# Packing the first attention's small matmuls into quarter tiles, and a new order at two seams

## The reference, cut to what matters

```
def _L0_xattn_ref(x, cond, ...):          # x, cond: (16, 64, 512): 64 channels, 512 positions
    HEADS, WINDOW = 8, 16                 # 8 channels a head
    q, k, v = Wq x + bq, Wk cond + bk, Wv cond + bv        # over the 64 channels
    k, v = padded by 8 positions on the left and 7 on the right
    # each position t attends to its window of 16 positions, t-8 .. t+7
    dots = einsum('bhdt,bhdtw->bhtw', q, k_windows) * 8 ** -0.5
    attn = softmax(dots)
    out = einsum('bhtw,bhdtw->bhdt', attn, v_windows)
    return Wo out + bo
x = x + _L0_xattn_ref(_layernorm(x), ctx, ...)
x = x + _L0_ffn_ref(_layernorm(x), ...)   # rounds its input to int8 steps, gate and up, silu, rounds, down
```

## Time and profile before

| | |
|---|---|
| median of 3 runs | 1571.63 us (1570.21 to 1572.16) |
| the profiled execution | 1569.83 us, its span 1568.0 us |
| busy in the span | PE 1493.3, DVE 820.6, ACT 749.3, POOL 502.2 us |
| instructions | 27690 |
| first attention | from about 12 us (first scores) to about 230 us |

### The profile page before, as it was taken

The page is one execution under the profiler, slowest core; times in us unless marked ns, Lnnn a source line. Parts: engine busy times, 40 slices in busy tenths (PEclk is TensorE's granted clock), DMA queues, the critical chain, the costliest instruction groups (busy, mean ns, idle before and its releaser), DMA issues. The chain is left out here.

```text
span 1568.0 us, 27690 instructions
## 1 busy us (share of the span) xinstructions
PE 1493.3 (95%) x10396; PEld 1240.2 (79%) x10402; DVE 820.6 (52%) x1682; ACT 749.3 (48%) x2552; POOL 502.2 (32%) x656
## 2 busy tenths in 40 slices
PE   7988979999999999999999998779999999999998
PEld 6777768888989888888889887656666778888876
DVE  4767875544444555544443457666665412343465
ACT  5645545454545445454544565355433312455552
POOL 6677652322222212222222224245322000123334
PEclk9999999999999999999999999999999999999999
DMA  8000010020100101010010110010100001122111
GB/s 256 10 9 15 2 41 29 30 73 28 41 27 4 38 28 42 28 41 28 7 36 28 41 55 1 21 64 0 41 1 0 9 23 55 47 70 80 46 27 63
DMA packets 44453, 58.20 MB, mean 37 GB/s; under 512 B 25488, under 2 KB 32672, under 8 KB 41504
## 3 DMA queue, kind: packets, MB, share of 16 engines
q1 hardware_dynamic: 43872, 56.05, 11.3%
q10 hardware_dynamic: 384, 0.38, 0.1%
q0 software_dynamic: 64, 0.00, 0.0%
HBM read 48.81 MB, written 2.10 MB: 32 GB/s over the span
## 5 line engine op out<-in xcount | busy, mean ns | idle before, releaser
L1862 ACT ACTIVATE big<-pb 128x128 f32<-128x128 f32 x384 | 106.7, 278 | 298.5 <-PE pb L902 195.8
L2232 POOL TENSOR_TENSOR big<-big 128x512 f32<-128x512 f32 x96 | 100.0, 1042 | 258.3 <-DVE big L1494 258.3
L1911 ACT ACTIVATE big<-pb,big 128x128 f32<-128x128 f32 x384 | 136.1, 368 | 57.0 <-issue 34.3
L1489 DVE TENSOR_REDUCE big<-pb 128x4 f32<-128x512 f32 x96 | 65.8, 686 | 176.1 <-PE pb L941 168.1
L917 PE MATMUL pb<-wkh,CXh 128*128 128x256 f32 x512 | 149.7, 292 | 0.0
L2222 POOL TENSOR_SCALAR big<-big 128x6 f32<-128x6 f32 x64 | 12.9, 202 | 412.8 <-ACT big L1862 412.2
L917 PE MATMUL pb<-wkl,CXh 128*128 128x256 f32 x512 | 145.0, 283 | 0.0
L917 PE MATMUL pb<-wkh,CXl 128*128 128x256 f32 x512 | 144.2, 282 | 0.0
L1280 DVE TENSOR_TENSOR X<-X,pb 128x512 f32<-128x512 f32 x128 | 87.0, 679 | 79.7 <-PE pb L1128 39.3
L968 PE MATMUL pb<-woh,oh 128*128 128x512 f32 x256 | 113.0, 442 | 0.0
L902 PE MATMUL pb<-wqh,CXh 128*128 128x512 f32 x256 | 101.8, 397 | 3.0 <-DVE big L1459 1.6
(11 more groups left out here) (283 smaller groups left out, 3872.7 us busy)
## 6 DMA issues: line engine op xcount, KB each, us to landing
big<-in_w SPq DMA_DIRECT2D x17, 1024.0 KB, 5.0
big<-in_w SPq DMA_DIRECT2D x24, 256.0 KB, 3.0
big<-in_w SPq DMA_DIRECT2D x8, 512.0 KB, 3.6
o<-o SPq DMA_DIRECT2D x96, 32.0 KB, 1.9
X<-in_x SPq DMA_DIRECT2D x8, 256.0 KB, 4.8
big<-in_cn SPq DMA_DIRECT2D x8, 256.0 KB, 3.0
CXlf<-in_cT SPq DMA_DIRECT2D x8, 256.0 KB, 5.1
big<-in_wa SPq DMA_DIRECT2D x1, 2048.0 KB, 8.6
```

The lines of the kernel that those rows point to most:

```text
L1489: v.tensor_reduce(m[j % 2], quarters(bank(p)), AX, MAX, negate=True).then_inc(S.m, 1)
L1862: y = a.activation(sq[i % 2], bank(p)[:, j * width:j * width + 128], ACT.Square, accum_out=ss[i % 2][:, first + j:first + j + 1])
L1911: y = a.activation(e_[:, c], bank(p)[:, c], ACT.Exp, bias=m[j % 2][:, k:k + 1], scale=1.0, accum_out=z[j % 2][:, k:k + 1])
L2232: g.tensor_tensor(quarters(e_), quarters(e_), bc(r[j % 2], 128), MUL).then_inc(*on.to(S.pn))
```

## The change

The list `l0` gets two PE stages, `l0_half` and `l0_second`, around `l0_turn`. Together they compute the scores of unit u and the values of unit u+1 as matmuls of 64x64: in the first half, 8 of the scores on the diagonal quarters and 8 of the values off it; in the second half the other way round. The other engines' stages `l0_scores` and `l0_project` keep their places; PE does `l0_project` only for unit 0. The weighing takes the heads one by one (32 matmuls with 32 columns of weights and 32 moving columns in place of 16 with 64 and 64), so that only 128 columns of a bank are filled and copied; the output takes two heads at a time (2 matmuls in place of 4). The two pipeline steps of the feed-forward block stand at 9 and 11 of the longer list, ahead of `l0_scores` and of `l0_norm` as before. Stages of `ffn1` get `first`: `f1_stats`, `f1_norm`, `f1_turn` and `f1_mm` come ahead of `l2_turn`, `l2_rows`, `l2_stats` and `f1_quant` in their pipeline step. Weights, masks and their host layout follow (channels in another order); two bias products on ACT go.

```diff
-    l0 = [("l0_mask", 2), ("l0_rows", 1), ("l0_out", 7), ("l0_sum", 4), ("l0_ctx", 7), ("l0_weigh", 6), ("l0_turn", 5),
-          ("l0_scores", 3), ("l0_project", 2), ("l0_norm", 0), ("l0_qk", 1)]
+    l0 = [("l0_mask", 2), ("l0_rows", 1), ("l0_out", 7), ("l0_sum", 4), ("l0_ctx", 7), ("l0_weigh", 6), ("l0_half", 3),
+          ("l0_turn", 5), ("l0_second", 3), ("l0_scores", 3), ("l0_project", 2), ("l0_norm", 0), ("l0_qk", 1)]
...
-    ffn1 = pipeline([3 * t for t in range(NT)], [(s, None if s == "f1_wait" else every) for s in f1])
+    ffn1 = pipeline([3 * t for t in range(NT)], [(s, None if s == "f1_wait" else every) for s in f1],
+                    first=("f1_stats", "f1_norm", "f1_turn", "f1_mm"))
...
-            together(next(att0), (ffn0, 7), (ffn0, 9))
+            together(next(att0), (ffn0, 9), (ffn0, 11))
...
-        together(first[:7], (late, 6), (ffn0, 7))
+        together(first[:9], (late, 7), (ffn0, 9))
...
+            halves = slice(0, 64), slice(64, 128)
+
+            def pad_values(u):
+                g, p = u % 4, PSUM["l0_project", u, "v"]
+                return pe.matmul(bank(p)[:, g * 128:g * 128 + 128], pad[0:16, g // 3 * 128:g // 3 * 128 + 128],
+                                 pad[0:16, 256:384], start=False, stop=True, skip_group_check=True)
+
+            def values(u, k, rows_, keys, first):
+                n = rows_ * 16
+                return pe.matmul(view(bank(PSUM["l0_project", u, "v"])[halves[keys]], k * 128 + n, [[32, 4], [1, 16]]),
+                                 CP[u % 3][halves[rows_], k * 128 + keys * 64:k * 128 + keys * 64 + 64],
+                                 view(wv0[halves[rows_]], n, [[32, 4], [1, 16]]), start=first, stop=True,
+                                 skip_group_check=True)
+
+            def scores(u, i, rows_, out_):
+                t, g = divmod(u, 4)
+                return pe.matmul(bank(PSUM["l0_scores", u, "S"])[halves[out_], i * 64:i * 64 + 64],
+                                 Qx[u % 2][halves[rows_], i * 64:i * 64 + 64],
+                                 view(K0[t % 2][halves[rows_]], (8 * g + i) * 16, [[560, 2], [1, 32]]), start=False,
+                                 stop=True, skip_group_check=True)
+
             def l0_project(u):
-                t, g = divmod(u, 4)
+                if u:
+                    return
                 on.wait_ge(D.w0, 16)
                 on.wait_ge(D.pad, 16)
                 p = PSUM["l0_project", u, "v"]
-                C_ = CP[u % 3]
                 on.wait_ge(S.cp, 2 * u + 2)
                 on.wait_ge(p.free, p.n)
                 for k in range(4):
-                    a = pe.matmul(bank(p)[:, k * 128:k * 128 + 128], C_[:, k * 128:k * 128 + 128], wv0,
-                                  start=(k == 0), stop=True, skip_group_check=True)
-
-                if g in (0, 3):
-                    a = pe.matmul(bank(p)[:, g * 128:g * 128 + 128], pad[0:16, g // 3 * 128:g // 3 * 128 + 128],
-                                  pad[0:16, 256:384], start=False, stop=True, skip_group_check=True)
-                a.then_inc(p.full, 1)
-
-            def l0_scores(u):
+                    pe.matmul(bank(p)[:, k * 128:k * 128 + 128], CP[u % 3][:, k * 128:k * 128 + 128], wv0,
+                              start=(k == 0), stop=True, skip_group_check=True)
+                pad_values(u).then_inc(p.full, 1)
+
+            def l0_half(u):
                 t, g = divmod(u, 4)
                 p, k = PSUM["l0_scores", u, "S"], PSUM["l0_qk", 4 * t, "k"]
                 on.wait_ge(S.qx, u + 1)
                 on.wait_ge(k.free, k.n + 1)
                 on.wait_ge(S.band, 2)
                 on.wait_ge(p.free, p.n)
-                halves = slice(0, 64), slice(64, 128)
                 for r in halves:
                     pe.matmul(bank(p)[r], bandb[r, 0:64], bandb[r, 128:640], start=True, stop=False, skip_group_check=True)
-                for i in range(8):
-                    for r in halves:
-                        a = pe.matmul(bank(p)[r, i * 64:i * 64 + 64], Qx[u % 2][r, i * 64:i * 64 + 64],
-                                      view(K0[t % 2][r], (8 * g + i) * 16, [[560, 2], [1, 32]]), start=False,
-                                      stop=True, skip_group_check=True)
-                a.then_inc(p.full, 1)
+                if u + 1 < 4 * NT:
+                    v = PSUM["l0_project", u + 1, "v"]
+                    on.wait_ge(S.cp, 2 * u + 4)
+                    on.wait_ge(v.free, v.n)
+                for i in range(4):
+                    for r in range(2):
+                        a = scores(u, i, r, r)
+                        if i == 3:
+                            a.then_inc(S.half0, 1)
+                    for r in range(2):
+                        if u + 1 < 4 * NT:
+                            a = values(u + 1, i, r, 1 - r, i == 0)
+                            if i == 3:
+                                a.then_inc(S.half0, 1)
+
+            def l0_second(u):
+                p = PSUM["l0_scores", u, "S"]
+                on.wait_ge(S.half0, 4 * u + (4 if u + 1 < 4 * NT else 2))
+                for i in range(4):
+                    for r in range(2):
+                        a = scores(u, 4 + i, r, 1 - r)
+                    if i == 3:
+                        a.then_inc(p.full, 1)
+                    for r in range(2):
+                        if u + 1 < 4 * NT:
+                            a = values(u + 1, i, r, r, False)
+                if u + 1 < 4 * NT:
+                    if (u + 1) % 4 in (0, 3):
+                        a = pad_values(u + 1)
+                    a.then_inc(PSUM["l0_project", u + 1, "v"].full, 1)
 
...
                 for j in range(4):
                     for p, r in zip((p0, p1), halves):
-                        for c in halves:
-                            k = slice(j * 128 + c.start, j * 128 + c.stop)
-                            a = pe.matmul(bank(p)[c, j * 64:j * 64 + 64], VW[u % 4][r, k], PT0[u % 2][r, k],
+                        for h in range(4):
+                            c = j * 128 + 32 * ((h + j // 2 * 2) % 4)
+                            a = pe.matmul(bank(p)[32 * h:32 * h + 32, j * 32:j * 32 + 32],
+                                          VW[u % 4][r, j * 128 + 32 * h:j * 128 + 32 * h + 32], PT0[u % 2][r, c:c + 32],
...
-                for h in range(4):
+                for h in range(2):
                     a = pe.matmul(bank(p)[:, 0:128], wo0[:, h, :],
-                                  view(AV[u % 2], h * 16, [[64, 4], [256, 2], [1, 16]]), start=(h == 0), stop=(h == 3))
+                                  view(AV[u % 2], h * 16, [[32, 4], [128, 2], [1, 16]]), start=(h == 0), stop=(h == 1))
...
-                    a.copy(AV[u % 2][:, h * 256:h * 256 + 256], bank(p)[:, 0:256]).then_inc(p.free, 1)
+                    a.copy(AV[u % 2][:, h * 128:h * 128 + 128], bank(p)[:, 0:128]).then_inc(p.free, 1)
```

More of the change, by code:

```diff
@@ L414, in build_program @@
         S.zero, S.zp, S.two = sem("dve_constants"), sem("pool_constants"), sem("l0_wo_masked")
-        S.cp, S.qx, S.band = sem("l0_windows"), sem("l0_q_masked"), sem("l0_band")
+        S.cp, S.qx, S.band, S.half0 = sem("l0_windows"), sem("l0_q_masked"), sem("l0_band"), sem("l0_first_half")
         S.exp0, S.rc0, S.pn0 = sem("l0_exp"), sem("l0_reciprocal"), sem("l0_probs")
@@ L588, in build_program @@
         K0 = [b.rearrange("p (b n) -> p b n", b=2) for b in Kbd]
-        wo0 = al(4 * 128).rearrange("p (h n) -> p h n", h=4)
+        wo0 = al(2 * 128).rearrange("p (h n) -> p h n", h=2)
         bo0 = al(1)
@@ L592, in build_program @@
         al = carve(R1, R1 + 6144)
-        Qx, VW, AV = slots(al, 2, 512), slots(al, 4, 512), slots(al, 2, 512)
+        Qx, VW, AV = slots(al, 2, 512), slots(al, 4, 512), slots(al, 2, 256)
         al = carve(R1 + 6144, R1 + 10240)
@@ L599, in build_program @@
         pad, bandb = al(384), al(640, BF16)
-        wo_raw, band = CXf[0][:, 64:198], CXf[0][:, 2048:2688]
-        wob, bv0, hmo, bo_raw = wo_raw[:, 0:128], wo_raw[:, 128:129], wo_raw[:, 129:133], wo_raw[:, 133:134]
+        wo_raw, band = CXf[0][:, 64:196], CXf[0][:, 2048:2688]
+        wob, bv0, hmo, bo_raw = wo_raw[:, 0:128], wo_raw[:, 128:129], wo_raw[:, 129:131], wo_raw[:, 131:132]
         al = carve(RF, R0 + 22788)
@@ L1226, in f3_mm @@
                 a.then_inc(p.full, 1)
-            do = dict(l0_bias=l0_bias, l0_qk=l0_qk, l0_project=l0_project, l0_scores=l0_scores, l0_turn=l0_turn,
+            do = dict(l0_bias=l0_bias, l0_qk=l0_qk, l0_project=l0_project, l0_half=l0_half, l0_second=l0_second, l0_turn=l0_turn,
                       l0_weigh=l0_weigh, l0_out=l0_out, f0_turn=f0_turn, f0_turn_u=f0_turn_u, f0_gate=f0_gate, f0_turn2=f0_turn2, f0_down=f0_down,
@@ L2525, in diag @@
         return z
-    order = np.arange(128).reshape(2, 2, 32).transpose(1, 0, 2).reshape(128)
+    order = np.arange(128).reshape(2, 4, 16).transpose(1, 0, 2).reshape(128)
     p = np.arange(128)
```

(7 more changed lines are left out.)

## The result

The changed kernel takes 1611.12 us (median of 4 runs, 1606.5 to 1617.1) against 1570.92 for the kernel before on the same chip: ratio 1.0257, interval 1.0235 to 1.0278. It is slower, by 40 us where the forecast had 23; its median lies 2 to 3 us above the range (1577 to 1609 in the sum, 1576 to 1608 in the chances). The profiled execution's span is 1607.5 us.

A forecast was written before the change was run, and what follows sets the result against it. The prediction took the first feed-forward's ring across engines, not PE's busy share, as the bound; 1.8 + 19.2 + 7 - 5 = +23 us on 1571.63 gave 1594 us, range 1577 to 1609 (1576 to 1608 in the chances).

The forecast's parts named there:

- The bank-0 wait: First half of unit 4t+10 waits for ACT's quT copy out of bank 0: 3.2 us a tile, +19.2 us.
- The clock: PE stands still before quT's end, clock falls to half speed: 1.2 us a tile, +7 us (0 to 10).
- the 4.8 us: Predicted time from quT's end to DVE's gate step in each tile, against 1.3 us today.
- The start: First units' halves wait bare for ACT's copy of the values: +1.8 us (0.4 to 2.5).
- The seam: Near 1000 us, second feed-forward's stages go ahead of layer 2's turn: -5 us (-9 to +3).
- Saved TensorE time: PE work removed per attention unit: 1.3 us, 40 us over 31 units, counted as nothing.
- the ring: First feed-forward layer's closed loop through POOL, DVE, ACT and PE, once per tile, 29.1 us; said to set the time.
- Rival 1: PE is the bound after all: 15 us of the 40 and 5 from the seam gained, 1552; chance 0.09.
- rival 2: The waits are hidden by slack or earlier ACT copies; only start and seam count: 1568; chance 0.10.
- Weighing in 64 records: PE's new weighing in 32-column tiles: taken as 0.63 us; by record rate 1.26, by the skill page 1.6.
- the two waits: PE's halves wait for ACT's values copy in every unit (+1.8 us) and for quT in every tile (+19.2 us).

The follow-up runs named there:

- e4: The changed kernel with unread bf16 matmuls put into TensorE's longest standstills of the first attention, no wait removed: 1594.3 us, ratio 1.0145.
- e5: The changed kernel with l0_project ahead of l0_scores, so ACT copies the values before the exponential: 1604.0 us, ratio 1.0212.
- e1: The kernel before with only the order of stages in the second feed-forward's pipeline at the seam changed: 1566.5 us, ratio 0.9968.
- e9: The changed kernel with values copied before the exponential and both halves back to back where the scores stood: 1568.8 us, ratio 0.9984.
- e12: The changed kernel with only both halves moved back to back behind the turn and the feed-forward's stages: 1580.8 us, ratio 1.0067.
- e6: The changed kernel with values copied before the exponential and f0_turn_u of tiles 0 to 5 in bank 1: 1594.0 us, ratio 1.0148.
- e2: The changed kernel with f0_turn_u of tiles 0 to 5 in PSUM bank 1 in place of bank 0: 1589.1 us, ratio 1.0113.
- e7: e6 with unread bf16 matmuls ahead of f0_turn_u and of five weighings: 1581.5 us, ratio 1.0067.
- e11: e9 with unread bf16 matmuls in front of f0_turn_u's wait and of the first turn: 1571.5 us, ratio 0.9998.
- e8: The changed kernel with old score and value stages at their old places; new weighing, output and seam order kept: 1569.6 us, ratio 0.9987.
- e10: The kernel before with the new seam order and l0_project ahead of l0_scores, no packing, old weighing and output: 1575.3 us, ratio 1.0019.
- e3: The changed kernel with TensorE alone taking the gate and down products ahead of the next unit's first half: 1590.3 us, ratio 1.0124.

## Why the prediction was right in direction and wrong in size

- **The bank-0 wait, +19.2:** right. With the clock nearly held (e4, 0.97 from 60 to 230 us) a tile takes 32.2 us, 3.13 over before, 6 x 3.13 = 18.8. Part of that is the down product, which I left out, balanced by the slack at X += xg0.
- **The clock, +7 (0 to 10): the term that failed.** It measured 6 x (35.0 - 32.2) = 17. I let one fall a tile cover 3.4 of the 4.8 us and lose at most 1.7, although the fall in the earlier trace rows lasts 6.83 us. In four of six tiles the clock was at half for 6.8 to 10.2 us around the step, which lost 2.8 to 3.5; three of the six down steps ran slowly too (2.5 to 2.9 us for 1.6).
- **The start, +1.8: failed too.** It measured 8.5, and e5 gives 6 of it back, 4.2 of them at equal half clock. I followed DVE's and ACT's steps and took them to add nothing; unit 0's turn and the next queries and keys, queued on PE behind the waiting half, I did not follow, and I had no fall of the clock there. How the rest of the 8.5 divides stays open.
- **The seam, -5:** right (e1: 5.3 us less).
- **Saved TensorE time, 0:** right. In e9, with the halves out of the ring's way, the tile is 29.1 us as before, and the time saved is standstill. Rival 1 is out; so is rival 2, by the 17.4 us that PE waits for quT.
- **Weighing in 64 records, 0.63:** right (PE, kernel after, at full clock):

```profile
203.04 0.76 PE L875 MATMUL pb<-big 64*32 64x32 f32 x64
203.72 0.40 PE L822 MATMUL pb<-big 64*64 64x512 bf16 x2
```

  0.68 us from start to start, 10.6 ns a record. The Trainium skill (TensorE: Matmul & The Clock Gate, "Wait — 56ns, not 53.3ns?") has no matmuls closer than about 25 ns, by which 64 records would take an estimated 1.6 us. This trace, with eight of these tiles in the array, does not agree.

Sum by measurement: 8.5 + 18.8 + 17 - 5.3 = 39, for 40 measured (the first three are, by construction, the delay of tile 6, 275.7 - 231.6 = 44 us). The prediction had named the two waits; it priced most of what is queued behind them at full speed, and some of it at nothing.

## What to carry to other kernels

Where one engine's products close a ring, look at what stands ahead of them in its queue, not at its busy share: here the same packed stages cost 30 us more ahead of those products than behind them (e12), and behind them, with the values copied first, nothing that these runs show over the seam order alone (e9 against e1). Here work taken off an engine that is not in the ring turned into standstill, and on TensorE that cost clock; as a bound, price everything queued directly behind such a standstill at half speed (it came so in four of six tiles), not a part of it. And a wait that is taken away alone may only move on (e5, e6): follow the ring once around after each edit.

## What the runs showed of the hardware

In the kernel after, up to 290 us, the clock fell to 1.2 GHz twelve times, for 3.4 to 13.7 us. Seven times the last standstill of 1 us or more ahead of the fall was 1.3 to 3.1 us long; five times PE was still in one, of 2.6 to 4.2 us. Equal standstills kept the clock: PE stood 2.6 us for quT in tile 0 and 2.3 us in tile 4, and both kept it through the gate step. What decides is open.

In e2, e4 to e7, e9, e11 and e12 PE also stands for 2.0 to 3.1 us once or twice between 27 and 42 us, in the middle of a run of packed matmuls with no wait among them. e4, and the queue q8 of the DMA table in that standstill (29.35 to 32.42; packets, MB, share):

```profile
32.42 0.21 PE L789 MATMUL pb<-big 64*64 64x64 f32 x1 [3.07 <-issue]
```
```profile
q8 instruction: 1, 0.02, 2.6%
```

No semaphore accounts for it, and the kernels with the old score and value stages (before, e1, e8, e10) have none; the kernel after and e3 have shorter ones, of 0.8 to 1.5 us. Two counts point at PE's own instructions. In each of these standstills PE has 691, 943 or 1197 matmuls and weight loads behind it, steps of 252 and 254, also in e4, which has unread matmuls among them. And q8 moves one 16 KB packet per 251 of them (96 packets for 24084 in the kernel after, 83 for 20798 before); one starts between 0.4 us before and 0.7 us after the start of each of these standstills (e4: 29.82). So PE most likely stood until its next instructions were loaded; no run tests it. The standstills lie ahead of these kernels' first products (61.0 in e9, with 3.1 us of it). A second bank for the values, which would take the unit's wait away without a new order, was not tried: no bank is free.
